# Attention scores: three fp32r products of high and low parts against one plain fp32 product on each 64-row half

## The reference, cut to what matters

```python
xn = layernorm(x, ln_x_g, ln_x_b)              # 4096 context rows of 256
ln = layernorm(latents, ln_l_g, ln_l_b)        # 256 latent rows of 256
q  = (ln @ Wq)                                 # 16 heads of 64
kv = concatenate([xn @ Wkv, ln @ Wkv], axis=1) # keys and values of 4352 rows
qn = rmsnorm(q, qn_g) * scale
kn = rmsnorm(k, kn_g)
sim  = einsum('bhid,bhjd->bhij', qn, kn)       # the scores
attn = softmax(where(mask, sim, -max))
out  = einsum('bhij,bhjd->bhid', attn, v)
x = x + out.reshape(b, m, h * d) @ Wout + bout
```

## Time and profile before

| | |
|---|---|
| median of 3 runs | 781.3 us (780.48 to 782.1) |
| the profiled execution | 780.73 us |
| its span, first to last instruction | 779.0 us |
| busy: PE, PEld, DVE, ACT, POOL | 91%, 74%, 70%, 56%, 29% |
| share of full TensorE clock granted, mean | 0.945 |
| attention, first projection to last exit | 65.4 to about 606 us |
| a usual step of attention | 3.74 us |

### The profile page before, as it was taken

How to read it: one execution, slowest core, us unless ns; L and a number is a source line. 1 busy time by engine, 2 the same in 40 slices (tenths; PEclk the granted TensorE clock), 3 DMA queues, 4 the chain that set the end, 5 groups by cost and what they waited for, 6 DMA issues and landing times. The chain is left out here.

```text
span 779.0 us, 15876 instructions
## 1 busy us (share of the span) xinstructions
PE 706.3 (91%) x5910; PEld 575.5 (74%) x5910; DVE 541.9 (70%) x1012; ACT 439.8 (56%) x985; POOL 226.8 (29%) x194
## 2 busy tenths in 40 slices
PE   1537999999999999999999999999998775799998
PEld 1436777777777777777777777777775664799997
DVE  5995777677767767777776776777776452666764
ACT  4445666666666666666665665666564321456552
POOL 3531332232223223223222322322221020164460
PEclk9958999999999999999999999999999655699999
DMA  6205300000000000000000000000000300455610
GB/s 192 80 30 142 99 1 3 1 21 2 1 22 1 2 1 21 2 1 22 2 2 21 2 2 1 9 1 2 2 1 1 109 1 4 159 163 174 203 54 15
DMA packets 27562, 30.61 MB, mean 39 GB/s; under 512 B 4313, under 2 KB 24930, under 8 KB 27490
## 3 DMA queue, kind: packets, MB, share of 16 engines
q1 hardware_dynamic: 24834, 28.26, 11.5%
q10 hardware_dynamic: 2656, 1.39, 0.6%
HBM read 29.38 MB, written 0.26 MB: 38 GB/s over the span
## 5 line engine op out<-in xcount | busy, mean ns | idle before, releaser
L837 POOL TENSOR_TENSOR k_rms<-k_ss,neg_half 128x4 f32<-128x4 f32 x136 | 136.9, 1007 | 379.7 <-DVE k_ss L784 379.7
L528 PEld LDWEIGHTS kv_ps<-w_pair,xn 128*128 128x128 f32 x1632 | 202.5, 190 | 52.8 <-issue 52.7
L528 PE MATMUL kv_ps<-w_pair,xn 128*128 128x256 f32 x1632 | 229.9, 290 | 5.1 <-PEq L179 5.1
L777 DVE SCALAR_TENSOR_TENSOR sum_ps<-probs,tile_mask,sum_ps 128x512 f32<-128x512 f32 x256 | 193.3, 755 | 19.0 <-ACT probs L725 1.7
L725 ACT ACTIVATE probs<-s_ps,minus_bound 128x512 f32<-128x512 f32 x272 | 172.2, 684 | 4.9 <-PE s_ps L636 2.3
L701 ACT ACTIVATE k_sq<-kv_ps 128x256 f32<-128x256 f32 x136 | 52.1, 383 | 191.4 <-PE kv_ps L528 191.4
L648 PE MATMUL o_ps<-probs,v 128*64 128x256 f32 x1088 | 147.5, 392 | 0.4 <-ACT probs L725 0.4
L636 PE MATMUL s_ps<-q_parts,kt 64*128 64x256 f32 x1632 | 131.2, 293 | 0.5 <-ACT probs L725 0.5
L636 PEld LDWEIGHTS s_ps<-q_parts,kt 64*128 64x128 f32 x1632 | 104.2, 184 | 23.6 <-issue 22.7
L648 PEld LDWEIGHTS o_ps<-probs,v 128*64 128x64 f32 x1088 | 66.1, 136 | 37.8 <-ACT probs L725 0.8
L788 DVE TENSOR_TENSOR kt<-kt_ps,kt 128x256 fp32r<-128x256 f32 x136 | 57.7, 424 | 49.3 <-ACT kt L717 49.2
(11 more groups left out here) (183 smaller groups left out, 676.5 us busy)
## 6 DMA issues: line engine op xcount, KB each, us to landing
w_raw<-in_ffn_W SPq DMA_DIRECT2D x18, 1024.0 KB, 5.3
p_rows<-in_ctx SPq DMA_DIRECT2D x8, 512.0 KB, 3.8
w_raw<-in_L_xattn_Wkv SPq DMA_DIRECT2D x14, 128.0 KB, 2.4
p_wq_raw<-in_L_xattn_Wq ACTq DMA_DIRECT2D x1, 1024.0 KB, 5.9
wout<-in_L_xattn_Wout SPq DMA_DIRECT2D x8, 128.0 KB, 2.1
x_res<-in_x SPq DMA_DIRECT2D x1, 256.0 KB, 4.4
w_raw<-in_L_xattn_Wkv ACTq DMA_DIRECT2D x2, 128.0 KB, 4.0
f_Wq<-in_L_attn_Wq SPq DMA_DIRECT2D x1, 256.0 KB, 3.7
```

What stands on the lines that cost most here:

```text
L528: last = nc.tensor.matmul(out, stationary(k, s), moving(k, m), start=n == 0, stop=n == len(terms) - 1)
L777: nc.vector.scalar_tensor_tensor(total[:], probs[n % 2][:, i], seen, sum_ps[:], ALU.mult, ALU.add).then_inc(sum_done, 1)
L837: nc.gpsimd.tensor_tensor(k_rms[n % 2][:].rearrange("p i c -> p (i c)"), k_ss[n % 2][:].rearrange("p i c -> p (i c)"), neg_half[:, 0:4], A ...
```

## The change

The queries and K^T are kept once, in plain fp32, and each score tile is one plain fp32 matmul. The low-part instructions of K^T (136 on DVE) and of the queries (4 on DVE) are gone, and PE waits for ACT's copy (`kt_kept`) instead of DVE's subtraction.

```diff
-            q_parts = hold("q_parts", [P, NPASS, 2, NQ], F32R)
+            q_t = hold("q_t", [P, NPASS, NQ])
@@ prepare, ACT
-                nc.scalar.activation(q_parts[:, 2 * c:2 * c + 2, 0, :], qt_of(c), ACT.Copy, scale=gqk_col[:]).then_inc(qt_hi, 1)
+                nc.scalar.activation(q_t[:, 2 * c:2 * c + 2, :], qt_of(c), ACT.Copy, scale=gqk_col[:]).then_inc(qt_kept, 1)
@@ prepare, DVE
-            def qt_lo_part(c):
-                dve.wait_ge(qt_hi, c + 1)
-                nc.vector.scalar_tensor_tensor(q_parts[:, 2 * c:2 * c + 2, 1, :], qt_of(c),
-                                               gqk_col[:], q_parts[:, 2 * c:2 * c + 2, 0, :].bitcast(F32),
-                                               ALU.mult, ALU.subtract).then_inc(qt_lo, 1)
@@
             normalise(8, rows[2])
-            qt_lo_part(0)
             lo(7)
-            qt_lo_part(1)
-            qt_lo_part(2)
             lo(8)
-            qt_lo_part(3)
@@ attention
-        kt = ring(2, "kt", [P, 2, 2 * P], F32R)
+        kt = ring(2, "kt", [P, 2 * P])
@@ attention, PE
             def transpose_k(n):
                 pe.wait_ge(kn_done, n + 1)
                 if n:
-                    pe.wait_ge(kt_lo, n)
+                    pe.wait_ge(kt_kept, n)
@@
             def scores(n):
                 g, b = n // NU, n % 2
-                pe.wait_ge(kt_lo, n + 1)
+                pe.wait_ge(kt_kept, n + 1)
                 if n:
                     pe.wait_ge(exp_done, 2 * n)
                 for i in range(2):
-                    for t, (s, m) in enumerate(((0, 0), (0, 1), (1, 0))):
-                        for c in range(2):
-                            half = slice(c * DH, (c + 1) * DH)
-                            last = nc.tensor.matmul(s_ps[c][:, i, :], kt[b][half, s, i * P:(i + 1) * P],
-                                                    q_parts[half, g, m, :], start=t == 0, stop=t == 2)
-                            if i == 1 and t == 2:
-                                last.then_inc(s_done, 1)
+                    for c in range(2):
+                        half = slice(c * DH, (c + 1) * DH)
+                        last = nc.tensor.matmul(s_ps[c][:, i, :], kt[b][half, i * P:(i + 1) * P], q_t[half, g, :], start=True, stop=True)
+                        if i == 1:
+                            last.then_inc(s_done, 1)
@@ attention, ACT
-                nc.scalar.activation(kt[n % 2][:, 0, :], kt_ps[:, 0:2 * P], ACT.Copy).then_inc(kt_hi, 1)
+                nc.scalar.activation(kt[n % 2][:], kt_ps[:, 0:2 * P], ACT.Copy).then_inc(kt_kept, 1)
@@ attention, DVE
-            def kt_rest(n):
-                dve.wait_ge(kt_hi, n + 1)
-                nc.vector.tensor_tensor(kt[n % 2][:, 1, :], kt_ps[:, 0:2 * P], kt[n % 2][:, 0, :].bitcast(F32), ALU.subtract).then_inc(kt_lo, 1)
@@
-                if exists(n + 1):
-                    kt_rest(n + 1)
```

More of the change, by code:

```diff
@@ L160, in perceiver_kernel @@
             xn = hold("xn", [P, NT, KD, 2, P], F32R)
-            prepare(nc, sem, a, x_res, ident, ones, neg_half, w_raw[0], w_pair[0], q_parts, tile_mask, minus_bound, xn)
-            attention(nc, sem, a, x_res, ident, ones, neg_half, w_raw, w_pair, q_parts, tile_mask, minus_bound, xn, fw, ew)
+            prepare(nc, sem, a, x_res, ident, ones, neg_half, w_raw[0], w_pair[0], q_t, tile_mask, minus_bound, xn)
+            attention(nc, sem, a, x_res, ident, ones, neg_half, w_raw, w_pair, q_t, tile_mask, minus_bound, xn, fw, ew)
         with ExitStack() as scope:
@@ L167, in perceiver_kernel, with prepare @@
         store_result(nc, sem, out, x_res)
-def prepare(nc, sem, a, x_res, ident, ones, neg_half, w_raw, w_pair, q_parts, tile_mask, minus_bound, xn):
+def prepare(nc, sem, a, x_res, ident, ones, neg_half, w_raw, w_pair, q_t, tile_mask, minus_bound, xn):
     groups = NG + 1
@@ L220, in prepare @@
             sem("q_done"), sem("q_sq_done"), sem("q_ss_done"), sem("q_ms_done"), sem("q_rms_done"), sem("qn_done"))
-        qt_done, qt_hi, qt_lo, col_done = sem("qt_done"), sem("qt_hi"), sem("qt_lo"), sem("col_done")
+        qt_done, qt_kept, col_done = sem("qt_done"), sem("qt_kept"), sem("col_done")
         def parts_of(n):
@@ L529, in part_products, with attention @@
     return last
-def attention(nc, sem, a, x_res, ident, ones, neg_half, w_raw, w_pair, q_parts, tile_mask, minus_bound, xn, fw, ew):
+def attention(nc, sem, a, x_res, ident, ones, neg_half, w_raw, w_pair, q_t, tile_mask, minus_bound, xn, fw, ew):
     V_RING = 4
@@ L561, in attention @@
         kv_done, sq_done, ss_done, rms_done = sem("kv_done"), sem("sq_done"), sem("ss_done"), sem("rms_done")
-        v_kept, kn_done, kt_done, kt_hi, kt_lo = sem("v_kept"), sem("kn_done"), sem("kt_done"), sem("kt_hi"), sem("kt_lo")
+        v_kept, kn_done, kt_done, kt_kept = sem("v_kept"), sem("kn_done"), sem("kt_done"), sem("kt_kept")
         s_done, exp_done, sum_done, pv_done = sem("s_done"), sem("exp_done"), sem("sum_done"), sem("pv_done")
```

## The result

The changed kernel takes 805.5 us (median of 4 runs, 801.4 to 806.3) against 780.9 us for the kernel before: 1.0302 times as long, 95% interval 1.0264 to 1.034. The forecast was 802.0 us.

A forecast was written before the change was run, and what follows sets the result against it. PE's own chain was taken to bound the attention. From 780.73 us, +22.0 for the scores and -0.7 for the queries, with nothing for K^T's low part, waits and projections, gave 802.0 us, ratio 1.027; range 795 to 810.

The forecast's parts named there:

- Bound: Attention: PE's own work fills the 3.74 us step, and PE waits for no other engine to speak of.
- Scores, four slots: Attention's score block: eight fp32 records in four paired slots, 1.058 us against 0.895, +0.163 a step, +22.0 us in all.
- Projection slots: Attention's projection block: taken as 0; up to 8 us less if the shorter block became usual, kept in part for the range.
- Low part of K^T: Attention: removing 136 DVE instructions, 57.7 us, is worth nothing, as DVE idles over 1 us in each step.
- Queries: End of `prepare`: without DVE's fourth low part the stage ends earlier, -0.66 us, between 0 and -0.7.
- step sum: Whole kernel: 780.73 us before, + 22.0 for the scores, - 0.7 for the queries, gives 802.0 us.
- One slot more: Score block: matmuls start strictly in program order, five slots instead of four, +0.38 us a step, 831 us; chance 5%.
- halves one after another: Score block: the array's halves don't overlap in fp32, eight slots, 1.92 us, +139 us, 919 us in all; chance 3%.
- The first weight loads: Score block: the two halves' first weight loads run one after another, +0.27 us a step, 816.5 us; chance 4%.
- The rival on the other side: Score block: faster than before if an fp32 slot is under 0.175 us; at 0.117 the time is 748.7 us; chance 2%.

The follow-up runs named there:

- Both experiments on DVE: DVE's subtraction kept in the changed kernel: 802.3 us; all low parts removed from the kernel before, its three products all taking high parts: 780.8 us.
- the heads in turn: The changed kernel with the two score loops exchanged, both row tiles of head 0 and then both of head 1: 806.4 us, ratio 1.0322.
- the second series: The changed kernel, not edited, measured again beside the experiments: 802.7 us (802.6 to 803.0), ratio 1.0271.

## Why the prediction was right

- *Bound.* Right: PE's own chain, with under 2 us of waits in the whole loop before and after. Both experiments on DVE show that it isn't DVE.
- *Scores, four slots.* Right in the mechanism, and nearly in size: `project_out` gave 1.058 us for the block, it took 1.064, so +0.169 a step instead of +0.163: 22.8 us instead of 22.0. The 0.006 us are the second head's records, which trail the first head's by 7 ns (by 13 ns with the heads in turn, where the block took 1.071); in `project_out`, on one half, nothing trails. The decomposition that gave it (0.195 plus slots) also gave the block on one half (1.92 us measured, 1.93 worked out) and, within 0.02 us, that of four products (1.15 against 1.13).
- *Projection slots.* The term taken as zero was mis-sized, and its tail had the wrong sign: I kept 8 us for a projection that gets quicker, and the 14 quick ones of before were lost, 14 x 0.05 = +0.7 us. With it the attention's growth is 23.5 us, and measured are 23.3 and 24.0. Why they were quick isn't settled. They are lost as well with the heads in turn, with four and with two products and with DVE's work kept, though `project_out` ahead of them is the same. One is left with both heads on one half, 7 with two products and one copy of K^T, and all 14 with DVE's work taken away alone. DVE's low part by itself doesn't decide it: taking it away changes nothing with three products, and brings 7 back with two. It may be a matter of phase between engines; no run tells.
- *Low part of K^T*: nothing, right. *Queries*: -0.66 us in both pairs of traces, counted from the last low parts of rows, right.
- *The rest of the distance* lies outside the step sum. The profiled execution took 806.3 us, 4.3 above the forecast: 2.0 in the attention, 1.8 in the store's landing, 0.4 outside the span. That the second series, at 802.7 us, comes within 0.7 us of the forecast is in part luck: in its trace the attention took 1.3 us more than forecast and began 1.2 later, and the random-feature attention, at a higher granted clock, took 2.7 less. A forecast from one execution can't be closer than these.
- *Rivals.* One slot more and halves one after another were told apart from the forecast by experiments, not only by the trace of after. The first weight loads run side by side: the second starts 7 ns after the first, and the first two records end within 0.49 us, where one alone has up to 0.48. The rival on the other side, an fp32 slot under 0.175 us, fell with the slot of 0.213 to 0.216.

## What to carry to other kernels

Where PE is the bound, count streams of the moving operand. In these score blocks (64 rows, 128 columns of weights, 256 columns streamed) a plain fp32 matmul is two records, each with the time of two streams, and an fp32r one is one record with the time of one. So three fp32r products beat one fp32 product, and one fp32 product beats four. Price a new block from the nearest block of the same shape in the same trace, as slots by the distance of starts plus the filling and emptying at the change of shape, never by the duration of a record. Work taken off an engine that PE doesn't wait for brings nothing, however many microseconds of it the page shows; but once PE's own work has shrunk, look again at every place where PE needs that engine, also at those that come once in many steps.

## What the runs showed of the hardware that I had not expected

- Matmuls on different 64-row halves don't wait for each other in the program's order: with two instructions of head 0 ahead of it, head 1's first record started 0.013 us after head 0's first, and the block kept its four slots.
- One fp32 record of 256 columns (0.216 us a slot, the time of two streams) is cheaper than two fp32r records: four slots against eight make the block 1.064 us against 1.148.
- A projection of twelve fp32r records has two paces, 0.113 and 0.118 us a slot, at the same granted clock of 1.00; which one it takes depends on the program around it, and it was the same in the two traces of each of the two kernels that were traced twice.
